# Attention in a four-stage block: later Q and K projections in twos over quads one to four, their weights split some steps ahead

## What is computed

```python
q = (x @ Wq.T + bq).reshape(b, l, h, hd).transpose(0, 2, 1, 3)
k = (x @ Wk.T + bk).reshape(b, l, h, hd).transpose(0, 2, 1, 3)
v = (x @ Wv.T + bv).reshape(b, l, h, hd).transpose(0, 2, 1, 3)
scores = jnp.einsum('bhqd,bhkd->bhqk', q, k) / math.sqrt(hd)
causal = jnp.tril(jnp.ones((l, l), bool))
scores = jnp.where(causal, scores, -jnp.inf)
att = jax.nn.softmax(scores, axis=-1)
out = jnp.einsum('bhqk,bhkd->bhqd', att, v)
```

## Time and profile before

| | |
|---|---|
| median of three runs | 4295.83 us (4293.31 to 4297.06) |
| the profiled execution's own time | 4294.83 us |
| its span | 4293.1 us |
| TensorE busy | 3861.4 us (90%), mean granted clock 0.907 |
| VectorE, ScalarE, GpSimd busy | 2711.2, 1695.2, 1880.8 us |
| attention of the first batch, quads 0 to 7 | from about 128 to 474 us of the span |

### The profile page before, as it was taken

How to read it: one execution, slowest core, us unless ns; L and a number is a source line. 1 busy time by engine, 2 the same in 40 slices (tenths; PEclk the granted TensorE clock), 3 DMA queues, 4 the chain that set the end, 5 groups by cost and what they waited for, 6 DMA issues and landing times.

```text
span 4293.1 us, 61464 instructions
## 1 busy us (share of the span) xinstructions
PE 3861.4 (90%) x18056; PEld 2813.5 (66%) x18056; DVE 2711.2 (63%) x5034; ACT 1695.2 (39%) x3538; POOL 1880.8 (44%) x2017
## 2 busy tenths in 40 slices
PE   7899799689999999979878896996899999999797
PEld 4444478567777777757654444885677777777576
DVE  3567445577777777764435673555777777777644
ACT  1344411355545555541113444113555555555411
POOL 1111344355555655654311113443555556655542
PEclk8677899899999999989977767998999999999899
DMA  3221011011100111001032210110101001110010
GB/s 73 36 36 31 24 51 45 22 33 30 32 20 25 34 32 29 22 15 45 35 81 36 36 32 29 46 45 22 35 28 32 20 25 34 32 29 22 15 52 35
DMA packets 81456, 145.59 MB, mean 34 GB/s; under 512 B 16392, under 2 KB 18520, under 8 KB 81264
## 3 DMA queue, kind: packets, MB, share of 16 engines
q1 hardware_dynamic: 81264, 143.28, 12.9%
HBM read 113.08 MB, written 4.19 MB: 27 GB/s over the span
## 4 chain that ended last, share of the span: by engine, by line
PE 69%; issue 11%; DVE 7%; ACT 4%; POOL 3%; DVEq 2%; POOLq 2%; DMA 1%; SPq 1%; ACTq 0%
PE banks L492 15%; PE banks L493 14%; PE banks L494 14%; PE banks L832 4%; PE banks L671 4%; PE banks L652 3%; PE banks L628 3%; PE banks L825 2%; PE banks L845 2%; DVE conv L1344 2%; DVEq L1347 1%; PE banks L767 1%; PE banks L768 1%; POOL X L1509 1%; ACT conv L1005 1%
## 5 line engine op out<-in xcount | busy, mean ns | idle before, releaser
L1344 DVE SCALAR_TENSOR_TENSOR conv<-banks,cpar,conv 128x509 f32<-128x509 f32 (+2 forms) x576 | 428.2, 744 | 115.3 <-ACT conv L1005 100.9
L948 ACT ACTIVATE probs<-banks 128x1024 f32<-128x1024 f32 (+3 forms) x384 | 297.7, 810 | 309.4 <-PE banks L652 308.9
L1172 DVE TENSOR_TENSOR Y<-banks,Y 128x512 f32<-128x512 f32 x400 | 276.1, 691 | 188.1 <-PE banks L494 187.9
L1608 POOL TENSOR_SCALAR_AFFINE_SELECT probs<-probs 128x256 f32<-128x256 f32 x256 | 104.2, 408 | 645.8 <-ACT probs L948 645.5
L628 PE MATMUL banks<-stack_k,stack_q 48*128 48x512 f32 (+3 forms) x768 | 331.7, 502 | 59.3 <-DVEq L1218 19.8
L1672 POOL TENSOR_TENSOR state<-state,gt 128x512 f32<-128x512 f32 x112 | 133.5, 1192 | 500.4 <-PE banks L825 500.4
L492 PE MATMUL banks<-xhi,f_hi 128*128 128x512 f32 x800 | 322.6, 403 | 3.5 <-DVE xlo L1143 3.5
L492 PE MATMUL banks<-xhi,wx_hi 128*128 128x512 f32 x768 | 312.0, 406 | 14.4 <-DVE conv L1344 14.4
L493 PE MATMUL banks<-xhi,f_lo 128*128 128x512 f32 x800 | 319.9, 400 | 0.0
L494 PE MATMUL banks<-xlo,f_hi 128*128 128x512 f32 x800 | 319.4, 399 | 0.0
L494 PE MATMUL banks<-xlo,wx_hi 128*128 128x512 f32 x768 | 306.0, 398 | 0.0
(11 more groups left out here) (209 smaller groups left out, 10185.0 us busy)
## 6 DMA issues: line engine op xcount, KB each, us to landing
m_raw<-in_w_mamba SPq DMA_DIRECT2D x224, 256.0 KB, 2.6
f_raw<-in_w_ffn SPq DMA_DIRECT2D x50, 768.0 KB, 4.5
stack_q<-part_hi SPq DMA_DIRECT2D x128, 64.0 KB, 2.4
stack_k<-part_hi SPq DMA_DIRECT2D x128, 64.0 KB, 2.5
X<-in_x SPq DMA_DIRECT2D x4, 1024.0 KB, 6.5
wqk_raw<-in_w_attn SPq DMA_DIRECT2D x8, 512.0 KB, 3.5
stack_q<-part_lo SPq DMA_DIRECT2D x64, 64.0 KB, 2.4
stack_k<-part_lo SPq DMA_DIRECT2D x64, 64.0 KB, 2.5
```

Of the source, the lines that this page charges most:

```text
L948: act.activation(probs[n % 2][:, 2 * p:2 * p + 2, 0:w], banks[:, 2 * p:2 * p + 2, 0:w], ACT.Exp, scale=1.0 / HD ** 0.5).then_inc(exp_done[ ...
L1172: dve.tensor_tensor(Y[:, i, :], bank[6 + i % 2], Y[:, i, :], ALU.add).then_inc(f["dn_used"], 1)
L1344: r = dve.scalar_tensor_tensor(out=rest, in0=src[:, 0:HALF - lag], scalar=cpar[:, o:o + 1], in1=rest, op0=ALU.mult, op1=ALU.add)
```

## The change

Splits become items of the list of their own ("split_w"). Pair 0's stands ahead of everything, pair 1's before piece 9 of quad 0, pair 2's behind step 4 of quad 0, pair 3's behind step 4 of quad 2. The projections of pairs 2 and 3 stand in twos: use 0 and 1 behind steps 1 and 3 of quads 1 and 3, use 2 and 3 behind steps 1 and 3 of quads 2 and 4.

```diff
@@ attention_order @@
 
+            yield "split_w", 0
             for use in range(4):
                 yield "proj", 0, use
             for i in range(5):
                 yield "values_in", i
             for n in range(NP):
+                if n == 9:
+                    yield "split_w", 1
...
-                    if t % 2 and n < 8 and n % 2 and (t + 3) // 2 < NQ // 2:
-                        yield "proj", (t + 3) // 2, n // 2
+                    if 1 <= t < 5 and n in (1, 3):
+                        yield "proj", (t + 3) // 2, n // 2 + 2 * (t % 2 == 0)
+                    if t in (0, 2) and n == 4:
+                        yield "split_w", t // 2 + 2
@@ GpSimd's program @@
                     if what == "proj":
-                        f, use = arg
                         ring += 1
-                        if use < 3 and use > 0:
-                            continue
-                        if use == 3:
-                            wqk_last_use = ring
-                            continue
+                        wqk_last_use = ring
+                    elif what == "split_w":
+                        f, = arg
                         held(pool, wqk_in, (b * (NQ // 2) + f + 1) * 32)
                         if f > 0:
                             held(pool, ring_done, b * RING + wqk_last_use)
```

## The result

| | before | changed |
|---|---|---|
| median | 4296.44 us (4293.31 to 4315.62, 4 runs) | 4349.12 us (4346.96 to 4355.84, 4 runs) |
| ratio of the two | | 1.0119 (95% interval 1.0098 to 1.014) |
| profiled execution: own time, span | 4294.83, 4293.1 us | 4346.96, 4345.2 us |

The changed kernel is 1.2% slower, 53 us, as forecast. Each engine runs as many instructions as before, and the page's chain of work shows where the difference sits: SyncE's queue, 1% of the chain of before, is now 4% of it. Its copies (L372) are among the largest lines. The two rows are the changed kernel's chain by engine and its group of scores (idle time last, with its releaser).

The account below looks back on a forecast made before the run. TensorE, 69% of the chain, was taken to set the time, with SyncE's queue having 6.2 us of air. 98.6 + 50.1 + 75.8 = 224.5 us a batch, together +53.5 us, gave 4349 us; range 4320 to 4371.

Parts of the forecast that it names:

- The stall, the main term: Second parts of quads 2 and 4: maxima late behind 48 copies; 38.5 and 37.3 us, stalls of 13.5 and 12.3.
- The second parts of quads 1 and 3: Steps 4 to 11, freed of two projections each, fall from about 33 us to 25.0 us each.
- The wait for wqk_lo: TensorE's wait for Pool's split in quads 1 and 3 goes: 1.7 us each, 3.4 us a batch.
- theory B: For the early splits alone: the wait also cost TensorE its clock; gain 7.3 us a batch, about 4282 us.
- The first parts with projections: Steps 0 to 3 of quads 1 to 4, two projections each: 24.65 us each, 98.6 us a batch.
- The rest of the execution keeps its length: Everything outside quads 1 to 4 stays as long as before; no difference added to the sum.
- Rival 1 (the queue keeps up): SyncE's copy block takes under 18.3 us, maxima not late; +1 us a batch, 4298 us; chance 0.06.
- Rivals 2 and 3: TensorE clock kept in first parts: 2 without late queue, 4262 us, chance 0.04; 3 with late queue, 4320 us, chance 0.06.
- The rule weighed: SyncE's copies: the page's small initiation time would mean maxima not late; forecast held 48 copies issue-bound, 0.59 us each.

Follow-up runs that it names:

- the q copies early: Changed kernel with q copies issued once q projections are there, only k copies after the last projection; 4305.36 us, ratio 1.0015 to the kernel before.
- held-back queue: Kernel before, with SyncE held at the two copy blocks until step 2's values of quads 2 and 4 are done; 4350.71 us, ratio 1.0129.
- the changed kernel's other profile: Changed kernel, unchanged, profiled once more in another execution; 4335.85 us.
- the early splits alone: Kernel before with only the splits of pairs 2 and 3 moved, projections untouched; 4290.74 us, ratio 0.9972; measured again 4283.27 us, ratio 0.9946.
- dense work in the last quad: Changed kernel plus 12 unread dense matmuls behind step 1 of each batch's last quad; 4356.42 us, ratio 1.0128 to the kernel before.

## Why the prediction was right, point by point

- **The stall, the main term: right.** Forecast 38.5 and 37.3 us for the second parts of quads 2 and 4, measured 38.42 and 37.41 (38.12 and 37.09 in the second batch). TensorE's wait for the maxima was forecast at some 50 us and is 48.2; each long one at 12 to 14, and quad 3's is 11.16. The two directions are both shown: the lateness goes with a shorter block (the q copies early), and comes by itself with a held-back queue. Its price in the comparison of ratios is 45 us with the moved projections, and 55 us alone; of the latter, quads 1 to 4 account for 40 us.
- **The second parts of quads 1 and 3: right.** Forecast 25.0, measured 25.03 and 25.27. The closeness is luck: in the changed kernel's other profile quad 1's first and second part are these windows, and the forecast for the two was 24.65 and 25.0.

```profile
169.76:190.39 20.63, 18.65 (x87) 9.68 (x84) 10.79 (x32) 6.72 (x10) 3.27 (x8) 0.83 0.00 1
190.39:219.14 28.75, 26.80 (x141) 12.08 (x141) 19.01 (x60) 13.28 (x18) 3.26 (x8) 0.70 0.01 2
```

- **The wait for wqk_lo: right that it goes, its worth probably too small.** The term was 1.7 us each; in the early splits alone the first parts lost 2.9 us on average. The interval of that kernel's second measurement (0.9927 to 0.9965) is even beyond theory B, so more than this one wait may hang on it; the runs don't say what.
- **The first parts with projections: mis-sized.** The term was 24.65 us each, from two readings of before with the wait subtracted. Measured 22.51, 22.65, 22.84 and 22.68. Eight of them make some 16 us less than forecast. The step that failed is this term, the mean of two readings less the bare wait. The early splits alone, with the projections where they were, already bring these parts of quads 1 and 3 to 23.4 us. Why the parts are cheaper than the term stays open. The clock over the projections is part of it: the earlier trace rows have 0.55 for the first projection in quad 1, and in the changed kernel it is the first of these windows of wqk_hi, at 0.85. But the removed wait doesn't explain it, for with the same wait the first projection of a quad also ran at 1.00: quad 3's in the earlier trace rows, and 5 of the 12 in the three profiles that have the wait.

```profile
173.93:177.45 3.52, 3.08 (x8) 1.74 (x8) 0.00 (x0) 0.85 0.00 0
185.40:189.90 4.50, 3.91 (x8) 2.20 (x8) 0.00 (x0) 0.64 0.00 0
```

- **"The rest of the execution keeps its length": wrong in the profiled execution.** Quads 1 to 4 grew by 19.2 and 18.6 us a batch and not by 26.8; the span grew by 52.1 us all the same. The last quad is 11.85 us longer in the first batch (36.49 from 24.64) and 7.4 in the second, with its clock, and the other parts are 5 us shorter. That the median fell on the forecast within 1 us is therefore luck in part: a term too dear by 16 us met some 14 us that weren't in the sum. The changed kernel's other profiled execution, 13 us lower, lies inside the range too.
- **Rival 1 (the queue keeps up): not what happened, but its price was right.** It gave 4298 us, +2, for the case that the maxima aren't late; the q copies early made this case, +0.15% (-0.04% to +0.34%).
- **Rivals 2 and 3 (the clock is kept).** The first parts of the profiled execution, 22.7 us on average, lie nearer to these rivals' 21.75 us than to the forecast's 24.65, and in the other profile quad 1's took 20.63 us, below both. It didn't turn the sign, as the prediction said it couldn't with a late queue.
- **The rule weighed.** SyncE's issues of 48 copies took 32.06 us (240.44 to 272.50), 0.67 us each. The Trainium skill's page "DMA: Bandwidth & Descriptors", section "Issuing engines are not separate DMA queues", calls the time to initiate a DMA usually small relative to the DMA itself. For one copy the rows have a quarter of the time to landing; for 48 copies of 64 KB in a row the issues add up, and TensorE waited for what stood behind them. The prediction read the page as rival 1, a queue that keeps up; this reading is measured wrong here.

## What to carry to other kernels

Work that is moved takes its whole train of followers with it: ask which in-order queue the followers stand in, and what stands behind them. A queue that is idle for 70% of a stage can still be late, since what counts is the air between the end of its longest block and the next thing that someone waits for, here 6.2 us. And where the clock of TensorE falls differently from execution to execution, compare parts of several profiles before a difference of 1 to 10 us in one of them is explained. One forecast here was met within 0.03 us by a part that took 3.7 us more in the next profile.

## What the runs showed of the hardware

- **TensorE can stay at 1.2 GHz while it is busy all the time.** The last quad's second part had TensorE busy for 24.82 of 24.82 us at a granted clock of 0.50, and for 14.57 of 15.25 us at 1.00 in the kernel before. The Trainium skill's page "TensorE: Matmul & The Clock Gate", section "Part 1: The HAM clock gate", says that sustained work lifts the throttle; in this part, busy without a gap, it did not. In the 20.3 us form it did, late. These windows are the changed kernel's last quad in the second batch; the clock rises when TensorE has been busy throughout the first 13.54 of them:

```profile
2649.76:2663.30 13.54, 13.54 (x50) 4.83 (x49) 0.69 (x1) 7.76 (x8) 5.22 (x2) 0.50 0.00 0
2663.30:2670.10 6.80, 6.61 (x42) 2.74 (x40) 0.68 (x2) 4.85 (x8) 2.44 (x6) 1.00 0.00 0
```

  With 12 dense products ahead of the part (dense work in the last quad) the clock stood at 1.00 behind them in both batches, and in one of the two it fell again within the part.
- **The same part of the kernel differs in length from execution to execution.** The last quad's second part was 15.2, 20.3 or 24.7 to 24.8 us in all profiles; a second part without projections and without a stall 22.1 to 28.8 us. The 9.6 us between the shortest and the longest last quad, twice an execution, are by size nearly enough for the 24 us between the fastest and the slowest of 25 runs of the kernel before; that they make it up is not shown. Not every execution differs: the two profiles of the early splits alone agree in every part of quads 1 to 4 to 0.1 us.
- **The issue of a copy holds SyncE 0.59 us** at the median, for one of 64 KB (stack_k) and one of 16 KB (mt_lo) alike; some of the former take up to 1.66 us.
